# A two-layer decoder on one core: routing takes x and its rows' statistics from on-chip memory, with cross attention gathering the statistics

## The reference

```python
x = x + _L0_attn_ref(_layernorm(x), ...)                       # 16 heads of 64, causal, rotary
x = x + _L0_xattn_ref(_layernorm(x), ctx_1024, ctx_1024, ...)  # 16 heads of 32, causal
x = x + _L0_ffn_ref(_layernorm(x), gate_w, gate_b, w1, w2)     # 32 experts, below
x = x + _L1_attn_ref(...); x = x + _L1_xattn_ref(...); x = x + _L1_ffn_ref(...)

def _L0_ffn_ref(x, gate_w, gate_b, w1, w2):
    logits = jnp.einsum('bsd,ed->bse', x, gate_w) + gate_b
    probs = jax.nn.softmax(logits, axis=-2)                    # over the rows of a batch
    vals, idx = top_k(probs, 8 rows for each expert)
    merged = sum of the 8 chosen rows, weighted by vals        # (b, 32, 512)
    h = gelu([merged, 1] @ w1[e]);  o = [h, 1] @ w2[e]         # 512 -> 2048 -> 512 for each expert
    out = o, weighted by vals, added back to the chosen rows
```

## Time and profile before

| what | value |
|---|---|
| median of 3 runs | 3472.5 us (3468.34 to 3475.76) |
| the profiled execution's own time, its span | 3476.67 us, 3474.9 us |
| TensorE busy, share of the span | 3104.4 us, 89% |
| VectorE busy | 2102.6 us, 61% |
| ScalarE, GpSimd busy | 1396.0 us, 1324.5 us |
| cross attention | about 1098 to 1725.5 us |
| end of cross attention to the first product of the experts | 1725.5 to 1833.9 us |
| experts | to about 2500 us |
| granted TensorE clock, mean | 0.951 |

### The profile page before, as it was taken

How to read it: one execution, slowest core, us unless ns; L and a number is a source line. 1 busy time by engine, 2 the same in 40 slices (tenths; PEclk the granted TensorE clock), 3 DMA queues, 4 the chain that set the end, 5 groups by cost and what they waited for, 6 DMA issues and landing times. The chain is left out here.

```text
span 3474.9 us, 72067 instructions
## 1 busy us (share of the span) xinstructions
PE 3104.4 (89%) x23816; PEld 2312.9 (67%) x23832; DVE 2102.6 (61%) x5257; ACT 1396.0 (40%) x4587; POOL 1324.5 (38%) x1995
## 2 busy tenths in 40 slices
PE   6999999999997999999768878787689996999997
PEld 5888888888885787788534433333367775676774
DVE  6676676676664878887662211111166676888885
ACT  4444444444443555555431111111021115777774
POOL 2454554554552444444310000000022224888786
PEclk9999999999997999999969998989989998999998
DMA  3001001001002111112169999999731113222221
GB/s 130 19 18 36 18 18 36 18 18 36 18 13 98 37 60 61 48 54 66 54 261 384 427 426 427 425 426 425 316 103 56 57 47 115 75 79 81 71 80 34
DMA packets 145833, 449.33 MB, mean 129 GB/s; under 512 B 11684, under 2 KB 63016, under 8 KB 125288
## 3 DMA queue, kind: packets, MB, share of 16 engines
q1 hardware_dynamic: 127848, 430.68, 32.1%
q10 hardware_dynamic: 17920, 17.83, 1.5%
HBM read 396.04 MB, written 52.43 MB: 129 GB/s over the span
## 5 line engine op out<-in xcount | busy, mean ns | idle before, releaser
L436 POOL TENSOR_TENSOR cross_prob<-cross_prob,cross_rsum 128x128 f32<-128x128 f32 (+1 forms) x512 | 255.5, 528 | 347.7 <-DVE cross_rsum L823 347.4
L436 POOL TENSOR_TENSOR self_prob<-self_prob,self_rsum 128x128 f32<-128x128 f32 (+1 forms) x512 | 284.8, 582 | 246.7 <-DVE self_rsum L823 246.6
L1833 POOL TENSOR_TENSOR last_prob<-last_prob,last_rsum 128x256 f32<-128x256 f32 x512 | 303.9, 624 | 115.2 <-DVE last_rsum L2169 113.0
L677 ACT ACTIVATE self_prob<-self_S,self_neg_max 128x128 f32<-128x128 f32 (+1 forms) x512 | 211.7, 425 | 201.1 <-DVE self_neg_max L815 201.0
L430 POOL TENSOR_TENSOR self_QK_T<-self_QK_T,self_turned 128x512 f32<-128x512 f32 x128 | 164.2, 1283 | 295.8 <-DVE self_QK_T L778 294.0
L1489 POOL MEMSET norm_minus_half<- 128x2 f32 x1 | 0.1, 99 | 687.9 <-POOLq L53 687.9
L2048 ACT ACTIVATE last_prob<-last_S,last_neg_max 128x256 f32<-128x256 f32 x512 | 237.5, 488 | 41.5 <-DVE last_neg_max L2165 41.5
L1258 PE MATMUL experts_H<-moe_w,experts_tok 128*32 128x512 f32 x1024 | 157.2, 752 | 93.5 <-DMA moe_b<-in_L_ffn_w 81.9
L677 ACT ACTIVATE cross_prob<-cross_S,cross_neg_max 128x128 f32<-128x128 f32 (+1 forms) x512 | 209.8, 428 | 76.3 <-DVE cross_neg_max L815 75.4
L1378 DVE COPY experts_hidT<-experts_T 128x512 f32<-128x512 f32 x32 | 22.1, 692 | 280.9 <-PE experts_T L1269 280.9
L1979 PE MATMUL last_T<-last_ident,last_prob 128*128 128x128 f32 x1024 | 168.2, 289 | 15.5 <-DVE last_probT L2174 12.6
(11 more groups left out here) (317 smaller groups left out, 9854.9 us busy)
## 6 DMA issues: line engine op xcount, KB each, us to landing
moe_w<-in_L_ffn_w SPq DMA_DIRECT2D x64, 4096.0 KB, 36.0
front_x_t<-in_x SPq DMA_DIRECT2D x16, 512.0 KB, 3.6
self_res<-in_x SPq DMA_DIRECT2D x16, 512.0 KB, 3.6
x<-self_res SPq DMA_DIRECT2D x16, 512.0 KB, 2.8
front_x_t<-x SPq DMA_DIRECT2D x16, 512.0 KB, 5.3
front_spare<-in_ctx SPq DMA_DIRECT2D x16, 512.0 KB, 6.1
cross_res<-x SPq DMA_DIRECT2D x16, 512.0 KB, 3.6
x<-cross_res SPq DMA_DIRECT2D x16, 512.0 KB, 2.8
```

The costliest lines, as they stand in the source:

```text
L436: ins = pool.tensor_tensor(pr, pr, rsum[:, h, t:t + 1].to_broadcast([P, KQ[t]]), ALU.mult)
L677: ins = act.activation(prob[:, h % NP, SOFF[t]:SOFF[t] + KQ[t]], SC[h % G][:, SOFF[t]:SOFF[t] + KQ[t]], ACT.Exp, bias=neg_max[:, h, t:t + ...
L1833: ins = pool.tensor_tensor(pr, pr, rsum[:, h, t:t + 1].to_broadcast([P, S]), ALU.mult)
```

## The change

- Cross attention gets a new VectorE step, `rows-`, as the last of its order: after the two output additions of batch r-1 it takes the mean and variance of the finished rows (two statistics instructions, a memset, two aggregations, a small copy into `late_mv`, which holds all 16 batches).
- SP, before it loads batch r into `cross_res`, waits for the landed store as before and now also for `rows-` (semaphore `row_kept`), since the new step still reads `cross_res`.
- In the pass r = 15 SP loads the finished batches 0 to 14 back into `late_x` (15 loads of 512 KB) with the gate's weights and bias; batch 15 is added straight into `late_x`, stored from there, and the phase does not wait for that store. `late_x` lies where the weights of expert 1 will lie; the four staged weights of cross attention use its second half at first.
- Routing does no statistics. One addition and one power over all 16 batches (128x32) replace 16 small ones; VectorE only normalises. ScalarE takes over the logits' copy and the copy into `merged` of groups 0 and 1 (groups 2 and 3 stay on VectorE); GpSimd takes over the eight subtractions for the split key and value weights; there are three transpose banks instead of two; `choose`, `merge` and `to_channels` of a group run later than before, beside the next groups' transposes.
- The constants of the experts phase, its first context batch and the zeroing of `tok` move into the route phase.

```diff
@@ ORDERS, cross0, DVE
-                "mask15 inv13 max15 O1- Q0+ z0 take10 mask0+ mask1+ max0+ inv14 take12 Q1+ max1+"),
+                "mask15 inv13 max15 O1- Q0+ z0 take10 mask0+ mask1+ max0+ inv14 take12 Q1+ max1+ rows-"),
@@ attention_phase, SP, pass r
-                if not isinstance(r, int) or r > 0:
-                    o = ("O", 1)
+                o = ("O", 1)
+                if not rotary and isinstance(r, int) and r == n_batch:
+                    sp.wait_ge(over.x_made, T)
+                    sp.dma_start(x_out[r - 1].rearrange("(t p) d -> p t d", p=P), over.x_of(r - 1)).then_inc(over.x_stored, 16)
+                elif not isinstance(r, int) or r > 0:
                     sp.wait_ge(a_free[BANK[o]], freed[BANK[o]].at(o, r - 1) + 1)
                     sp.dma_start(x_out[r - 1].rearrange("(t p) d -> p t d", p=P), res[:, :, :]).then_inc(stored, 16)
                     sp.wait_ge(stored, r * 16)
+                    if not rotary:
+                        sp.wait_ge(row_kept, r * 16)
                 if not isinstance(r, int) or 0 <= r < n_batch:
                     sp.dma_start(res[:, :, :], x_in[r].rearrange("(t p) d -> p t d", p=P)).then_inc(res_in, 16)
+                if not rotary and isinstance(r, int) and r == n_batch - 1:
+                    sp.wait_ge(w_lo, len(PIECES))
+                    for n in range(r):
+                        sp.dma_start(over.x_of(n), x_out[n].rearrange("(t p) d -> p t d", p=P)).then_inc(over.x_in, 16)
...
@@ attention_phase, DVE
+            def output_stats(n):
...
+                for t in range(T):
+                    dve.bn_stats(out_stats[:, t, :], rows[:, t, :]).then_inc(row_stats, 1)
+                dve.wait_ge(row_stats, n * 2 * T + T)
+                dve.memset(out_slot[:, :], 0.0)
+                for t in range(T):
+                    dve.bn_aggr(out_mv[:, t, :], out_stats[:, t, :]).then_inc(row_stats, 1)
+                dve.wait_ge(row_stats, n * 2 * T + 2 * T)
+                dve.tensor_copy(over.mv[:, at, :, :]..., out_mv...).then_inc(row_kept, 16)
...
@@ route, SP
-                sp.dma_start(x_of(0), x_in[0]...)          # and gateT, ident, gb, then 15 more batches of x
...
+                load_rows(0); load_rows(1); load_w1(sp, 0, 0)
+                sp.dma_start(rows...); sp.dma_start(fold...); sp.dma_start(bk_c...)
+                load_rows(2); load_rows(3); load_w2(sp, 0, 0)
+                store(0); load_rows(4); load_rows(5); store(1); load_rows(6); load_rows(7)
+                sp.wait_ge(m_full, NG // 2); load_w1(sp, 1, 1)
+                sp.wait_ge(kv_lo, 2 * KD); sp.dma_start(c_t, context(0)).then_inc(c_in, 16)
+                store(2); store(3)
                 sp.wait_ge(m_full, NG)
                 load_w2(sp, 1, 1)
...
@@ route, POOL
-                for n in range(n_batch):
-                    pool.wait_ge(ln, 5 * n + 5)
-                    pool.tensor_tensor(rstd[:, n % 2, :], rstd[:, n % 2, :], minus_half[:, :], ALU.pow).then_inc(ln_pow, 1)
+                pool.tensor_tensor(rows_of, rows_of, minus_half[:, :], ALU.pow).then_inc(ln_pow, 1)
+                pool.memset(tok[:, :, :, :], 0.0).then_inc(zeroed, 1)
+                for i in range(2 * KD):
+                    pool.wait_ge(kv_hi, i + 1)
+                    pool.tensor_tensor(kv_w[i // KD][1]..., kv_stage[:, i % 2, :], kv_w[i // KD][0]..., ALU.subtract).then_inc(kv_lo, 1)
@@ route, PE
                 for n in range(n_batch):
                     g = n // G - 1
                     transposes(n)
-                    if g >= 0 and n % G == 2:
-                        choice(g)
-                    if g >= 0 and n % G == 3:
-                        merge(g)
+                    if g >= 1 and n % G == 0:
+                        merge(g - 1)
+                    if g >= 1 and n % G == 1:
+                        to_channels(g - 1)
                     if n % G == 3:
                         logits(n // G)
                         if g >= 0:
-                            to_channels(g)
+                            choice(g)
```

More of the change, by code:

```diff
@@ L997, in _, with store @@
+                load_rows(0)
+                load_rows(1)
+                load_w1(sp, 0, 0)
+                sp.dma_start(rows[:, :, :], consts["rows"]).then_inc(rows_in, 16)
+                sp.dma_start(fold[:, :], consts["fold"]).then_inc(rows_in, 16)
+                sp.dma_start(bk_c[:, :], bk).then_inc(bk_in, 16)
+                load_rows(2)
+                load_rows(3)
                 load_w2(sp, 0, 0)
-                for g in range(NG):
+                def store(g):
                     sp.wait_ge(step, N_STEP * (g + 1))
```

236 lines of the change are left out of this document (129 added, 107 removed).

## The result

The changed kernel takes 3550.8 us (median of four runs, 3548.51 to 3553.74) against 3472.5 before (median of four runs by now, 3468.34 to 3475.76): 1.0222 times as long, 95% interval 1.021 to 1.0234. The forecast was 3513 with a range to 3548: the direction was right, the size too small by 38 us. The profiled spans are 3474.9 and 3548.2 us, 73.3 apart.

The account below looks back on a forecast made before the run. TensorE was taken to bound cross attention, a chain of waits the stretch behind it, transfers the experts. +84.4 us (cross attention) - 44 (routing) = +40.4: profiled 3476.7 to 3517, median 3513 us; range 3474 to 3548.

Parts of the forecast that it names:

- The wait on SP: Cross attention: SP's new wait delays the next x load, so TensorE loses 4.9 us a turn, 13 times.
- The rival in which x is in time: Cross attention: x arrives in time, only the step's own work is paid; 3440 us, faster; chance 0.10.
- The clock: Cross attention: after each stall TensorE runs at half speed for a while, 1.5 us a turn (0 to 2.6).
- The step's own work: Cross attention: of the new statistics step's 1.76 us on VectorE, 0.8 us reach TensorE in each turn.
- Cross attention: The whole phase: stall, clock and the step's work together add 84.4 us (57 to 113).
- Start of routing: Cross attention's end to first normalisation: 7.7 us, the phase turn 1.4 of it, the 15 x loads hidden.
- The power: Start of routing: GpSimd's one power over 32 columns takes 4 us (0.7 to 11).
- The groups: Routing's four groups: VectorE is far ahead, ScalarE's work and standing set the pace; 45.1 us (36 to 68).
- The tail: Routing, last logits to its end: same chain with warmer matmuls and the third group's merge in gaps; 10.5 us.
- The first product: Routing's end to the experts' first product: `bk_c` is already there, so 1.3 us instead of 10.6.
- Sum: Whole kernel: 84.4 us more in cross attention less 44 gained up to the experts, +40.4 us.

Follow-up runs that it names:

- x_first: The changed kernel with SP issuing the next x and context loads ahead of its wait for the finished rows' statistics: 3464.1 us, ratio 0.9974.
- wait_only: The changed kernel without the statistics work in cross attention, keeping the small copy, the semaphore and SP's wait: 3522.0 us, ratio 1.0143.
- gap_early: The changed kernel with the changes of x_first and rows_in_gap, and late x 0 to 13 and the gate loaded at pass 15's start: 3439.0 us.
- choose_late: gap_early_pow with VectorE's choice of a group moved behind the normalisation of the next group's fourth batch: 3429.5 us, ratio 0.9871.
- gap_early_pow: gap_early with GpSimd's one power of 32 columns cut into 16 powers of two columns: 3436.1 us, ratio 0.9893.
- rows_in_gap: The changed kernel with `rows-` moved behind take10, into VectorE's idle gap, SP's order as changed: 3440.5 us, ratio 0.9913.
- constants_only: The kernel before with only the experts' small constants (rows, fold, bk_c) loaded in the route phase: 3475.7 us, ratio 1.0003.
- best: The changed kernel with `rows-` behind take10, late x 0 to 13 and gate loaded before pass 15's store, powers per batch, later choice: 3429.6 us.

## Why the prediction was right in kind and wrong in size

- **The wait on SP: right.** 13 turns, x issued 0.93 us behind the reload and read 4.0 to 6.2 us later (forecast 5.3), a standing time of TensorE of 4.7 us in a turn where the prediction had 4.9. The rival in which x is in time needed under 3.3 us. x_first made it come true, and took 3464 us, not the rival's 3440: by its trace cross attention is 21 us longer than before instead of 12, and the join 32 us shorter instead of 44.
- **The clock: the term that failed in cross attention.** The step "of the first 5 us behind PV2- some 3 would be matmul work, done at half speed: 1.5 us a turn", with 2.6 as its bound. It measured 3.2 us a turn (41.4 us over 13), above even the bound. Both factors were too small. The low level holds for 8.7 us of a turn in the mean (113 over 13), where I had read 5 from the gap in the experts (there it held from 2115.7 to 2122.5, but TensorE stood for the first 1.5 us of it). And of that time TensorE is busy for some 6.4 (twice the 3.2), where I had put 3 of 5. The second was in the trace of the kernel before, where the first 5 us behind PV2- hold 4.34 of matmul work:

```profile
1574.60:1579.60 5.00, 4.34 (x51) 2.93 (x48) 4.70 (x18) 3.48 (x14) 2.48 (x5) 1.00 0.00 0
```

That is 13 x 1.7 = 22 us, and the shorter standing gives 3 back. The Trainium skill ("TensorE: Matmul & The Clock Gate", HAM oscillation) tells of a loop whose wait for a transfer brings the slow clock back in every pass. The trace agrees: all 13 turns have a stretch at 1.2 GHz, and the 13 of x_first, without the wait, have none.
- **The step's own work: 0.8 against 1.5 us a turn** (x_first). In the sum its delay of TensorE lies inside the stall, as predicted. But the work also holds the reload back by its own length: without it (wait_only) the kernel is 29 us faster.
- **Cross attention: 102.5 us against 84.4**, within the bounds of 57 to 113.
- **Start of routing: failed.** "The 15 loads of x [...] issued in pass 15 with a whole pass of work still ahead: hidden." They stand in the code of pass 15, but behind that pass's store, wait and reload: they start some 11 us before the end of cross attention, and their issuing alone takes SP 14.47 us. The phase turn took 7.67 us instead of 1.4, and gap_early took 5.65 us of such a wait away. I had priced the bytes, and not the queue's place and its 0.96 us a load.
- **The power: 5.43 us against 4**, within 0.7 to 11. To the first normalisation in all 15.3 us against 7.7.
- **The groups: 54.5 us against 45.1.** The first was 12.3 against 10.2, the next two 15.6 and 14.7 against 9.9 and 12.5, the last 12.0 against 12.5. "VectorE has no statistics left and is far ahead" is the step that failed: it is ahead in work and behind in order. choose_late took 7.9 us of the groups' 53.7 (gap_early_pow) away with that alone. Its 45.8 are near the forecast's 45.1, but in sum only: its groups take 12.2, 12.7, 11.3 and 9.6 where the forecast had 10.2, 9.9, 12.5 and 12.5. A part is the clock, too: in the changed kernel the third group's logits take 3.63 us for 32 matmuls at a clock of 0.52; in rows_in_gap, where that group ran at 1.00, they took 1.93 and the group 12.2 us:

```profile
1774.07 1.93 PE L1215 MATMUL route_L<-route_xT,late_gateT 128*32 128x256 f32 x32 [0.80 <-ACT route_xT L1141]
```

- **The tail: 9.0 us against 10.5. The first product: 2.75 against 1.3.** The reason given (`bk_c` alone) was half of it. By constants_only that half by itself is worth nothing; the change also moved the context batch, which my 1.3 us did not argue for. Right by luck there.
- **Sum:** 18.1 us too little for cross attention and 17.0 too much gain for routing, both to the same side, 35.1 us together. From the experts on, where the forecast had no change, the trace has 2.4 us less. That is 32.7 of the 32.9 us by which the spans miss the forecast (73.3 against 40.4). The medians miss it by 38, since the profiled execution of the kernel before lay 4.2 us above its median and that of the changed one 0.8 below.

## What to carry to other kernels

A wait added to an in-order queue is paid by the next thing behind it that is due: list what stands behind, with the slack of each, and put the work that releases the wait into a gap of its engine, or put the urgent loads ahead of the wait. Price a stall of TensorE as the stall plus what the lower clock takes until it is back, read as busy time over the same matmuls; here it was two thirds as much again. Where several transfers stand between two phases, moving one of them may be worth nothing until the last of them has moved.

## What the runs showed of the hardware

- **GpSimd's power goes by columns.** 128x2 takes 0.69 us and 128x32 5.43: (5.43 - 0.69) / 30 = 0.16 us a column and some 0.4 fixed, if it is a straight line (two widths were measured). In gap_early_pow the powers of 128x2 take 0.68 to 1.81 us, the long ones beside VectorE's normalisations.
- **More work can take less time.** 768 more matmuls in cross attention made the kernel 28 us faster, as TensorE stayed at 2.4 GHz through the stall in eight of 13 turns and was back sooner in the others.
- **Turns of a waiting loop differ.** Turns without a stall agree within 0.1 us (37.52 to 37.60), turns with one spread over 3 us (43.93 to 46.90). The wait for x differs by 2.2 us among them (2.92 to 5.12), and the time at the low clock is about 7 or about 10 us.
- **A VectorE step of two inputs took three times as long beside GpSimd.** VectorE in the changed kernel, all four such steps (ns, least, median, most) and one of them, then GpSimd at that time:

```profile
L1112 DVE TENSOR_TENSOR route_pr<-route_pr,route_rest x4: 424/1286/1515, 1858.9 to 1901.0; 128x256 f32<-128x256 f32 x4
```

```profile
1875.21 1.51 DVE L1112 TENSOR_TENSOR route_pr<-route_pr,route_rest 128x256 f32<-128x256 f32 x1
```

```profile
1875.18 1.27 POOL L1083 TENSOR_TENSOR moe_wvl<-front_spare,moe_wvh 128x512 fp32r<-128x512 f32 x1 [13.72 <-ACT moe_wvh L1184]
```

The 0.42 us step is the last, at 1901, where GpSimd does nothing. The other three (1.36, 1.51 and 1.21 us) each end 0.27 to 0.29 us behind the end of a subtraction of GpSimd. The step goes with its neighbour in the runs looked at: in the kernel before and in constants_only, where VectorE does these subtractions itself, all eight take 0.42 to 0.43 us; in choose_late and in best, three of the four start with no subtraction running and take 0.42 to 0.43, and the one that starts behind a running one takes 1.52. The Trainium skill ("SBUF — State Buffer", SBUF: two separate sides) has the two engines share a port pair that one of them holds for a whole instruction, the other waiting. The trace agrees, as far as times can show it. The changed kernel loses some 2.8 us to it in its three steps.
